# Writing u behind the first two maxima of a step in place of behind the fourth

## What is computed

```
conv[n] = sum_m c**(n-m) x[m] + last_conv * c**(n+1)     # complex c per channel, 32 steps
x = layernorm(x + real(conv) * x)                        # = layernorm((real(conv) + 1) * x)
x = layernorm(x + attention(x, ctx))                     # 16 heads of 16, relu on q, k, v, its own layer norm
ids = argmin(dist(rms_norm(x), centroids))               # one of 8 experts
x = layernorm(x + (x + expert[ids](rms_norm(x))))
```

## Time and profile before

| | |
|---|---|
| median of 3 runs | 1206.01 us (1204.95 to 1211.37) |
| the profiled execution | 1200.62 us |
| its span, first to last instruction | 1198.9 us |
| PE busy | 1109.3 us, 93% |
| DVE busy | 959.3 us, 80% |
| POOL busy | 770.7 us, 64% |
| ACT busy | 668.3 us, 56% |
| granted TensorE clock, mean | 0.988 |
| chain that ended last, shares | PE 39%, DVE 35%, issue 10%, POOL 7%, DMA 5%, SP's queue 2%, ACT 2% |

### The profile page before, as it was taken

The page is one execution under the profiler, slowest core; times in us unless marked ns, Lnnn a source line. Parts: engine busy times, 40 slices in busy tenths (PEclk is TensorE's granted clock), DMA queues, the critical chain, the costliest instruction groups (busy, mean ns, idle before and its releaser), DMA issues.

```text
span 1198.9 us, 27888 instructions
## 1 busy us (share of the span) xinstructions
PE 1109.3 (93%) x8314; PEld 826.7 (69%) x8315; DVE 959.3 (80%) x2437; ACT 668.3 (56%) x1417; POOL 770.7 (64%) x933
## 2 busy tenths in 40 slices
PE   4999999999998999999999999989999999999996
PEld 3776666666666666666666666658788888888885
DVE  6569999999999999999999999887755555555553
ACT  4267777777776777777777777763222222222221
POOL 4747878888987998898889883255333333333333
PEclk9999999999999999999999999989999999999998
DMA  5767677766655656655656545213554444445442
GB/s 119 194 172 211 188 183 192 194 158 154 153 147 137 159 148 148 168 146 150 156 142 159 149 126 121 52 28 116 176 155 150 151 148 147 155 150 156 146 149 88
DMA packets 124097, 178.04 MB, mean 149 GB/s; under 512 B 13670, under 2 KB 111599, under 8 KB 117776
## 3 DMA queue, kind: packets, MB, share of 16 engines
q1 hardware_dynamic: 117456, 159.65, 50.4%
q0 software_dynamic: 6528, 16.99, 4.7%
HBM read 124.47 MB, written 53.03 MB: 148 GB/s over the span
## 4 chain that ended last, share of the span: by engine, by line
PE 39%; DVE 35%; issue 10%; POOL 7%; DMA 5%; SPq 2%; ACT 2%; POOLq 0%; DVEq 0%; ACTq 0%
DVE neg_max_sb L1556 14%; PE Y L488 10%; PE G L450 8%; PE A L450 8%; DVE oq L1755 4%; DVE u L1574 4%; PE GT L460 2%; POOL buckets L849 2%; POOL state L805 2%; DMA neg_max<-nm_row 2%; PE M L1186 2%; PE S L1229 2%; DVE stx L1540 2%; DVE st L1540 2%; DVE row L1663 1%
## 5 line engine op out<-in xcount | busy, mean ns | idle before, releaser
L1556 DVE TENSOR_REDUCE neg_max_sb<-S 128x2 f32<-128x512 f32 x512 | 327.5, 681 | 33.0 <-PE S L1229 32.4
L1019 ACT ACTIVATE probs<-T 128x512 f32<-128x512 f32 x512 | 278.1, 595 | 135.7 <-PE T L1242 121.0
L1229 PE MATMUL S<-k_st,q_st 48*128 48x256 f32 x1024 | 208.1, 311 | 32.7 <-DVE neg_max_sb L1556 30.2
L1229 PEld LDWEIGHTS S<-k_st,q_st 48*128 48x128 f32 x1024 | 140.8, 185 | 102.6 <-issue 69.8
L1242 PE MATMUL T<-q_st,k_st 49*128 49x256 f32 x1024 | 204.4, 311 | 5.6 <-DMA q_st<-neg_max 2.3
L428 ACT ACTIVATE gT<-GT 128x512 f32<-128x512 f32 x71 | 42.5, 598 | 205.4 <-PE GT L460 202.1
L1242 PEld LDWEIGHTS T<-q_st,k_st 49*128 49x128 f32 x1024 | 140.8, 185 | 20.6 <-ACT probs L1019 13.2
L408 POOL DMA_INDIRECT out<-res,token x71 | 76.0, 1071 | 102.0 <-DVE res L575 97.0
L1178 PE MATMUL O<-probs,v_aug 128*32 128x256 f32 x2048 | 139.7, 391 | 0.7 <-ACT probs L1019 0.7
L488 PE MATMUL Y<-dn_sb,gT 128*128 128x256 f32 x568 | 134.5, 379 | 1.5 <-DMA dn_sb<-in_L_ffn_down_w 0.8
L849 POOL DMA_INDIRECT buckets<-row,slot x64 | 67.1, 1049 | 84.4 <-DVE slot L1810 73.5
(11 more groups left out here) (212 smaller groups left out, 2587.9 us busy)
## 6 DMA issues: line engine op xcount, KB each, us to landing
dn_sb<-in_L_ffn_down_w SPq DMA_DIRECT2D x71, 512.0 KB
k_st<-k_pieces SPq DMA_DIRECT2D x64, 256.0 KB, 3.7
q_st<-q_pieces SPq DMA_DIRECT2D x64, 256.0 KB, 3.7
xr<-buckets SPq DMA_DIRECT2D x71, 129.0 KB
xt<-in_x SPq DMA_DIRECT2D x32, 256.0 KB, 6.4
ct<-in_ctx SPq DMA_DIRECT2D x32, 256.0 KB, 6.8
k_pieces<-k_hi SPq DMA_DIRECT2D x32, 256.0 KB
k_pieces<-k_lo SPq DMA_DIRECT2D x32, 256.0 KB
```

The lines of the kernel that those rows point to most:

```text
L1019: a_.activation(probs[:, h % 8].rearrange("p k t -> p (k t)"), T_ps[h % 2][:, :], ACT.Exp, scale=DH ** -0.5).then_inc(s["exp_ok"], 1)
L1229: last = t_.matmul(S_ps[h % 2][:, c * TOK:(c + 1) * TOK], q_st[h // HPC][base:base + STACK, h % HPC, c * P:(c + 1) * P], k_st[h // HPC][ba ...
L1556: v.tensor_reduce(neg_max[:, cur.mod(2), :, h], S_ps[h % 2][:, :].rearrange("p (c t) -> p c t", c=NTC), AX.X, ALU.max, negate=True).then_i ...
```

## The change

The block that writes u moves, inside VectorE's loop over heads, from behind maxima 2 and 3 (h == 3) to right behind maxima 0 and 1 (h == 0), ahead of `write_rows(b)`. Its three waits move with it. The statistics of u stay at h == 4. The instructions and their number stay the same, and no other engine's list changes.

```diff
                         if h % 2 == 0:
                             maxima(cur, h)
                             maxima(cur, h + 1)
-                        if h == 0 and active(b):
-                            write_rows(b)
-                        if h == 3 and active(nn):
+                        if h == 0 and active(nn):
 
                             wait(dve, "x1_ok", nn - 1, 2)
                             wait(dve, "conv", nn, 5)
                             wait_ring(dve, x_in[nn.mod(2)], nn, 2, 16)
                             v.scalar_tensor_tensor(u[:, :, :], state[:, 0], 1.0, xt[:, nn.mod(2)], ALU.add, ALU.mult).then_inc(s["u_ok"], 1)
+                        if h == 0 and active(b):
+                            write_rows(b)
                         if h == 4 and active(nn):
```

## The result

The changed kernel takes 1220.01 us in the median of its runs (1217.39 to 1224.54), where the kernel before took 1206.01 (1203.6 to 1211.37) beside it: a ratio of 1.0114, interval 1.0088 to 1.0140. It is 14 us slower. The forecast was 1207.0 with a range of 1195 to 1216, so the time lies outside. The profiled execution took 1217.39 us, against 1200.62 of the kernel before.

What follows compares the result with a forecast made beforehand. A ring passing between engines was taken as the bound, with GpSimd's chain ending last from rows to dist. The 1206.0 median plus 25 x 0.07 = 1.7 gave 1207.7, rounded down to 1207.0; range 1195 to 1216.

Steps and rivals of the forecast that it cites:

- the first part: Step from routed rows to VectorE's first routing operation, dist: 8.35 us, GpSimd's chain read as ending last, VectorE 0.13 behind.
- The collision at the new place: At the step's head, u and GpSimd's rstd2 power compete for SBUF: +0.52 or +0.32 us, against -0.45 at xw.
- VectorE first: At u's new place u gets SBUF before GpSimd's power: +0.07 us a step, +1.7 us in all; chance 0.38.
- Rival 3: Between dist and slot, the one-hot operation loses to GpSimd's next instruction in 8 more steps: +9 us, 1215; chance 0.16.
- the second part: Step from dist to slot, on VectorE: 8.76 us, which the change was said not to touch.

Runs made afterwards that it cites:

- a_rows: Changed kernel with u two blocks later, behind the routed rows but still ahead of maxima 2 and 3: 1214.86 us, ratio 1.0050.
- a_wait: Changed kernel with one more wait on GpSimd, so k_lo starts only after VectorE's one-hot operation: 1203.39 us, ratio 0.9980.
- b_wait: Kernel before the change with one more wait on GpSimd, so k_lo starts only after the one-hot operation: 1201.39 us, ratio 0.9966.
- b_short: Kernel before the change, second residual addition cut from 16 to 15 columns a head from the second item on: 1212.87 us, ratio 1.0036.
- b_lose: Kernel before the change, with the one-hot operation made to wait until the second residual addition is signalled: 1220.84 us, ratio 1.0097.
- a_fill: Changed kernel with six unused statistics operations, together 2.05 us, on VectorE where u used to stand: 1211.4 us, ratio 1.0025.
- b_conv: Kernel before the change, with k_lo waiting for the one-hot operation and GpSimd's last state addition ahead of the scatter: 1216.77 us, ratio 1.0074.
- a_klate: Changed kernel with TensorE's key projection held back until maximum 7 of its step is done: 1241.6 us, ratio 1.0297.

## Why the prediction was wrong

**The bound of the first part: right.** It was read that GpSimd's chain ends last in the first part, by 0.13 us. The profile after has VectorE idle 0.53 us ahead of dist, ended by GpSimd's dist; the forecast said 0.4 to 0.5. The 2.5 us that VectorE got back have gone into waits for scores: its idle time ahead of maxima is 75.2 us on the page after and 33.0 on the page before.

**The collision at the new place: right.** "VectorE first" was taken with a lead of 0.02 us. In the step above u and the power start in the same hundredth (415.79) and u gets SBUF: the power takes 1.25 for a forecast of 0.72 + 0.52 = 1.24, xw 1.18 for 1.64 - 0.45 = 1.19. By the Trainium skill's page "SBUF — State Buffer", section "SBUF: two separate sides", the pair is held for the whole instruction by whoever starts first. The trace agrees: in a_rows, where u starts behind the first power, that power stays at 0.72, and the later one that starts at 418.64, while u runs from 418.45, is the one that grows. The forecast +0.07 us a step is 0.08 in the step shown and in the median step, and 2.0 us in all between a_wait and b_wait, for 1.7. That u came first rested on 0.02 us, so that this branch was met and not the other is in part luck.

**Rival 3, the tie in the second part: the step that failed.** The mechanism, its place and the price of 1.1 us were in the prediction, with a chance of 0.16 and a size of 8 steps, and the sum that gave 1207.0 had nothing for it. It was 14 steps more (8 to 22). At the prediction's price that is 14 x 1.1 = 15.4 us; dist to slot grew by 12.9, 0.9 a race. Two things were wrong in it. The argument against it, that both engines start this part from GpSimd's dist as before, holds but proves nothing: between dist and the race lie 4 us in which TensorE's and ScalarE's results arrive, and these came earlier because of the very change that was made (ScalarE's k by 0.5 us). And the size was set at a doubling, where the prediction's own remark that such ties hang on hundredths allows all the steps to fall to one side. A tie read from a trace in which it falls both ways, 8 to 18, has to be given an outcome of "nearly all lost" with a real chance. That outcome by the prediction's own prices is 1207.7 + 18 x 1.1 = 1227.5 at its far end, and the range should have reached toward it.

**The base.** The profile of before took 5.4 us less than its median. The prediction said so and put differences on the median, which was the right way: from median to median the change costs 14.0 us, and the two profiles differ by 16.8.

**What stays open.** By which path the earlier work behind maximum 3 tips the race. In single steps the two cases look alike to hundredths: the addition ahead of the one-hot operation ends 427.14 - 426.64 = 0.50 us behind GpSimd's operation (L795) when it is won before, and 429.06 - 428.57 = 0.49 when it is lost after. Over all steps of one kernel those won have the later end, by some 10 ns: in the changed kernel 0.512 to 0.523 us where it is won and 0.486 to 0.506 where it is lost, in a_rows 0.509 to 0.520 and 0.478 to 0.508; in the kernel before the two overlap, with medians of 0.506 and 0.500. It is no fixed line, since b_short wins at 0.476 to 0.484. Whether the later end is a cause of the win or only goes with it is not shown. The runs show that the race is tipped and what it costs, not the signal or access that does it. The rows of the kernel before from which its two ends come, GpSimd's first, then VectorE's:

```profile
425.36 1.28 POOL L795 TENSOR_TENSOR state<-state,decay 128x512 f32<-128x512 f32 x1
426.60 1.77 POOL L868 TENSOR_TENSOR k_lo<-k,k_hi 128x512 fp32r<-128x512 f32 x1
...
426.01 1.13 DVE L1755 TENSOR_TENSOR oq<-o,qn 128x256 f32<-128x256 f32 x1
```

## What to carry to other kernels

When a small operation on the critical path stands beside a long one of the other engine on the same memory, look at the shortest, median and longest time of its line: two values far apart in steps that are otherwise alike point to a race, and an edit upstream, even one that only frees time, can move nearly all of it to the wrong side. Price such a race at all its occurrences before counting a gain of tenths elsewhere, and settle it with a wait that lets the small operation go first: it cost the long one some 0.7 us off the path and brought the changed kernel from 1.0114 to 0.9980. Then read the next bound before using the time gained; here the steps that stayed long were those with a lower granted TensorE clock.

## What the runs showed of the hardware

The race is lopsided. If the one-hot operation wins, k_lo takes 1.77 us; if k_lo wins, k_lo takes 1.68 and the one-hot operation 1.25 in place of 0.18. So GpSimd gains 0.09 us where VectorE loses 1.07.

Winning goes with being queued right behind the running instruction on the same engine, but doesn't follow from it: in b_lose, where the one-hot operation is taken up only once the addition is signalled, it loses 26 of 26; queued right behind the addition it wins or loses.

An operation a sixteenth shorter made a kernel 0.4% slower (b_short), and 53 us of useless work made another 0.9% faster (a_fill).

A GpSimd operation on 128x2 elements is held up by VectorE: the power takes 0.72 us alone and 1.25 behind u. The CAST to slot, a VectorE operation with one small input, is held up as well: 0.65 us in place of 0.16 beside GpSimd's addition in b_conv.

The mean granted clock of TensorE was lower in the kernels without lost races. As the median of all runs it is 0.984 in the changed kernel and 0.983 to 0.984 in the kernel before, but 0.978 in a_wait, 0.979 in b_wait and 0.963 in b_conv. It doesn't go with the races alone: a_klate, which loses 24, has 0.972. Every step of more than 23.6 us in a_wait, b_wait and b_conv has a mean granted clock of 0.87 to 0.94 (5, 8 and 12 steps of 26). The other steps have 0.98 to 1.00. In the long steps that were looked at closely the fall is short and deep: 0.50, the lower level of 1.2 GHz, from 412.69 to 417.00 in b_conv, and 0.57 from 204.39 to 207.39 in b_wait, with TensorE busy throughout both. What made it fall was not tested.
